# Merging an expert pair's second product with two float16 matmuls, with six product and four row buffers and two additions issued at other places

## The reference, cut to what matters

```python
x = x + xattn(layernorm(x), ctx, mask, Wq, Wk, Wv, Wo)
h = layernorm(x)
topk_idx, topk_w = gate(h)                      # 4 of 32 experts
buf[e, slot] = h rows that chose e              # the first CAP = 128 of them
hid = silu(buf @ w1) * (buf @ w3)
ob = hid @ w2                                   # per expert [128, 512]
out = x + sum(ob rows * topk_w) + (silu(h @ sg) * (h @ su)) @ sd
```

## Time and profile before

| what | value |
|---|---|
| median of 3 runs | 1669.8 us (1669.02 to 1671.42) |
| profiled execution, its own time | 1666.62 us |
| its span | 1664.9 us |
| PE busy | 1617.9 us, 97% of the span, 12194 matmuls and transposes |
| DVE, ACT, POOL busy | 1213.6, 820.1, 818.8 us |
| granted TensorE clock, mean | 0.99 of full speed |

### The profile page before, as it was taken

The page is one execution under the profiler, slowest core; times in us unless marked ns, Lnnn a source line. Parts: engine busy times, 40 slices in busy tenths (PEclk is TensorE's granted clock), DMA queues, the critical chain, the costliest instruction groups (busy, mean ns, idle before and its releaser), DMA issues. The chain is left out here.

```text
span 1664.9 us, 34808 instructions
## 1 busy us (share of the span) xinstructions
PE 1617.9 (97%) x12194; PEld 1155.4 (69%) x12194; DVE 1213.6 (73%) x3508; ACT 820.1 (49%) x2028; POOL 818.8 (49%) x1136
## 2 busy tenths in 40 slices
PE   8999999999999999999999999999999999899975
PEld 5767677777777777767677777777777777555532
DVE  7887676767677776767676778787877766577764
ACT  6664344435343444444443545454554433577763
POOL 3444544545363645454544554646555356344443
PEclk9999999999999999999999999999999999999988
DMA  8754433334343334333433454545454485599984
GB/s 258 175 142 79 83 83 78 83 74 94 71 96 71 87 68 101 69 80 72 90 76 85 96 103 93 112 90 112 92 115 78 97 291 185 140 277 291 299 248 69
DMA packets 394477, 204.12 MB, mean 123 GB/s; under 512 B 347824, under 2 KB 356016, under 8 KB 394304
## 3 DMA queue, kind: packets, MB, share of 16 engines
q1 hardware_dynamic: 380432, 180.27, 44.5%
q0 software_dynamic: 13312, 20.57, 6.4%
q10 hardware_dynamic: 560, 1.05, 0.2%
HBM read 87.15 MB, written 31.36 MB: 71 GB/s over the span
## 5 line engine op out<-in xcount | busy, mean ns | idle before, releaser
L958 ACT ACTIVATE arena<-arena,neg_max 128x256 f32<-128x256 f32 x512 | 253.7, 496 | 378.6 <-DVE neg_max L1265 378.6
L695 POOL TENSOR_SCALAR arena<-arena,prob_scale 128x256 f16<-128x256 f32 x384 | 183.5, 492 | 451.2 <-DVE prob_scale L1274 449.2
L1616 PE MATMUL ps_query<-xn_both,arena 128*128 128x256 f16 x1024 | 279.5, 273 | 1.4 <-DMA xn_both<-xn_half 1.4
L1617 PE MATMUL ps_query<-xn_both,arena 128*128 128x256 f16 x1024 | 279.4, 273 | 0.0
L1618 PE MATMUL ps_query<-xn_both,arena 128*128 128x256 f16 x1024 | 279.4, 273 | 0.0
L1265 DVE CUSTOM_DVE_ANT_0 arena<-ps_score,mask_add 128x256 f32<-128x256 f32 x512 | 186.5, 421 | 126.2 <-PE ps_score L1618 126.2
L1280 DVE SCALAR_TENSOR_TENSOR arena<-arena,prob_scale 128x256 f16<-128x256 f32 x384 | 233.5, 655 | 7.1 <-POOL arena L695 7.1
L1616 PE MATMUL ps_out<-arena,o_t 128*128 128x512 f16 x512 | 194.1, 379 | 2.1 <-DVE o_t L1285 2.1
L1617 PE MATMUL ps_out<-arena,o_t 128*128 128x512 f16 x512 | 194.0, 379 | 0.0
L1618 PE MATMUL ps_out<-arena,o_t 128*128 128x512 f16 x512 | 194.0, 379 | 0.0
L750 POOL DMA_INDIRECT slot_table<-entry,slot_at x128 | 133.9, 1046 | 48.1 <-issue 33.6
(11 more groups left out here) (320 smaller groups left out, 4064.8 us busy)
## 6 DMA issues: line engine op xcount, KB each, us to landing
arena<-w SPq DMA_DIRECT2D x96, 512.0 KB, 6.8
x_in<-x SPq DMA_DIRECT2D x15, 512.0 KB, 3.6
xn_rows<-xn_half SPq DMA_DIRECT2D x15, 512.0 KB, 3.0
out_rows_dram<-x SPq DMA_DIRECT2D x30, 256.0 KB, 2.3
ctx_in<-ctx_t SPq DMA_DIRECT2D x16, 256.0 KB, 3.0
weight_in<-wq SPq DMA_DIRECT2D x8, 512.0 KB, 5.4
weight_in<-wo SPq DMA_DIRECT2D x8, 512.0 KB, 4.7
arena<-arena SPq DMA_TRANSPOSE x256
```

The source lines that it names most:

```text
L695: pool.tensor_scalar(p_rows[:, c, 0, :], probs[:, c, :], prob_scale[:, c:c + 1], 1.0, ALU.mult, ALU.mult).then_inc(norm_hi, 1)
L958: act.activation(probs[:, c, :], probs[:, c, :], ACT.Exp, bias=neg_max[:, c:c + 1], scale=-1.0, accum_out=prob_sum[:, c:c + 1]).then_inc(e ...
L1616: pe.matmul(dst, a.hi, b.hi, start=start and n == 0, stop=False)
L1617: pe.matmul(dst, a.hi, b.lo, start=False, stop=False)
```

## The change

Four edits.

1. **The pair's second product as a float16 pair.** ACT, behind `scale_y` of every odd expert, copies `ps_out[1]` once more into `pair_y.hi`, in float16 and scaled by 16 over `EY_S` (`pair_y` is the attention's `o_t`, idle by then). DVE makes `pair_y.lo` in `pair_rest`, from `ps_out[1]` and `pair_y.hi`, behind `expert_ht_low` of the next even step. The merge is two float16 matmuls, by `hi` and by `lo`, and waits for `pair_lo`; so does `expert_down` of odd experts, which overwrites `ps_out[1]`. The match matrix is float16.
2. **Six product buffers, four row buffers.** `scale_y(e)` waits for the addition of e-6, and gathers run six experts ahead.
3. **Two additions at other places.** `add_shared(1)` stands right behind the load of the slot table, `add_shared(2)` behind two splits further down; both stood behind five gathers.
4. `match` writes its row numbers without the copy at its end (three instructions, not four).

```diff
+PAIR_S = 16.0
...
-        rows_in = [rows.bitcast(F16) for rows in (x_in[0][:, 0, :], x_in[0][:, 1, :], x_in[1][:, 0, :])]
+        rows_in = [rows.bitcast(F16) for rows in (x_in[0][:, 0, :], x_in[0][:, 1, :], x_in[1][:, 0, :], x_in[1][:, 1, :])]
...
         expert_y = [x1[:, t, :] for t in range(TB)] + [
-            xn2_half[:, t, :, :].rearrange("p h d -> p (h d)").bitcast(F32) for t in range(TB)]
+            xn2_half[:, t, :, :].rearrange("p h d -> p (h d)").bitcast(F32) for t in range(TB)] + [
+            both[:, :, :, :].rearrange("p h k t -> p (h k t)")[:, 2 * D:4 * D].bitcast(F32) for both in xn_both]
...
+        pair_y = o_t
...
             def gather(e):
-                if e >= 3:
-                    pool.wait_ge(pe_rows, e - 2)
+                if e >= 4:
+                    pool.wait_ge(pe_rows, e - 3)
...
+            add_shared(1)
             late_split(17)
             pool.wait_ge(in_table, 16)
...
-            for e in range(3):
+            for e in range(4):
                 gather(e)
             for k in (20, 21):
                 late_split(k)
-            for e in range(3, 5):
+            add_shared(2)
+            for e in range(4, 6):
                 gather(e)
             for k in (22, 23):
                 late_split(k)
-            add_shared(1)
-            add_shared(2)
...
-                if e >= 4:
-                    act.wait_ge(added, adds_done["x", e - 4])
-                else:
+                if e >= 6:
+                    act.wait_ge(added, adds_done["x", e - 6])
+                elif e < 4:
...
-                act.activation(expert_y[e % 4], ps_out[e % 2][:, :], ACT.Copy, scale=1.0 / EY_S).then_inc(scaled_y, 1)
+                act.activation(expert_y[e % 6], ps_out[e % 2][:, :], ACT.Copy, scale=1.0 / EY_S).then_inc(scaled_y, 1)
+                if e % 2:
+                    if e > 1:
+                        act.wait_ge(pe_merged, e // 2)
+                    act.activation(pair_y.hi, ps_out[1][:, :], ACT.Copy, scale=PAIR_S / EY_S).then_inc(pair_hi, 1)
...
+            def pair_rest(e):
+                dve.wait_ge(pair_hi, e // 2 + 1)
+                dve.scalar_tensor_tensor(pair_y.lo, ps_out[1][:, :], PAIR_S / EY_S, pair_y.hi, ALU.mult,
+                                         ALU.subtract).then_inc(pair_lo, 1)
...
                     expert_ht_low(e)
+                if e >= 2 and e % 2 == 0:
+                    pair_rest(e - 2)
...
             def merge(e):
                 pe.wait_ge(matched, e // 2 + 1)
-                pe.wait_ge(scaled_y, scaled_at(e + 1))
-                pe.matmul(ps_out[0][:, :], pair_match[e // 2 % 2], expert_y[(e + 1) % 4], start=False, stop=True).then_inc(
-                    pe_merged, 1)
+                pe.wait_ge(pair_lo, e // 2 + 1)
+                pe.matmul(ps_out[0][:, :], pair_match[e // 2 % 2], pair_y.hi, start=False, stop=False)
+                pe.matmul(ps_out[0][:, :], pair_match[e // 2 % 2], pair_y.lo, start=False, stop=True).then_inc(pe_merged, 1)
```

More of the change, by code:

```diff
@@ L254, in build @@
                                  for both in ctx_both))]
-        pair_match = [one_hot[:, :, :, :].rearrange("p t k e -> p (t k e)")[:, n * P:(n + 1) * P] for n in range(2)]
+        pair_match = [one_hot[:, :, :, :].rearrange("p t k e -> p (t k e)").bitcast(F16)[:, n * P:(n + 1) * P]
+                      for n in range(2)]
+        pair_y = o_t
         scratch = picked[:, :, :, :].rearrange("p t k e -> p (t k e)")
-        row_f, to_spare, hits, row_moved = scratch[:, 0:E], scratch[:, E:2 * E], scratch[:, 2 * E:2 * E + 1], \
-            scratch[:, 2 * E + 1:2 * E + 2]
+        row_f, to_spare, hits = scratch[:, 0:E], scratch[:, E:2 * E], scratch[:, 2 * E:2 * E + 1]
         second_rows = scratch[:, 3 * E:3 * E + E // 2].bitcast(U32)
@@ L283, in build @@
         scattered = [signal(f"scattered{n}") for n in range(2)]
-        gathered = [signal(f"gathered{n}") for n in range(3)]
+        gathered = [signal(f"gathered{n}") for n in range(4)]
         in_expert = [signal(f"in_expert{n}") for n in range(AHEAD)]
@@ L317, in build @@
         dve_own, pool_own = signal("dve_own"), signal("pool_own")
-        matched, pe_merged = signal("matched"), signal("pe_merged")
+        matched, pe_merged, pair_hi, pair_lo = (signal(n) for n in ("matched", "pe_merged", "pair_hi", "pair_lo"))
         CONSTS = 14
@@ L755, in gather @@
             def gather(e):
-                if e >= 3:
-                    pool.wait_ge(pe_rows, e - 2)
+                if e >= 4:
+                    pool.wait_ge(pe_rows, e - 3)
                 pool.indirect_dma_start(
-                    rows_in[e % 3], None, xn2_rows, bass.IndirectOffsetOnAxis(ap=table[:, e, 0:1], axis=0),
-                    bounds_check=N + CAP - 1, oob_is_err=True).then_inc(gathered[e % 3], 16)
+                    rows_in[e % 4], None, xn2_rows, bass.IndirectOffsetOnAxis(ap=table[:, e, 0:1], axis=0),
+                    bounds_check=N + CAP - 1, oob_is_err=True).then_inc(gathered[e % 4], 16)
             def add_rows(e):
@@ L768, in add_rows @@
                 pool.indirect_dma_start(
-                    out, bass.IndirectOffsetOnAxis(ap=rows, axis=0), expert_y[e % 4], None,
+                    out, bass.IndirectOffsetOnAxis(ap=rows, axis=0), expert_y[e % 6], None,
                     bounds_check=N + 2 * CAP - 1, oob_is_err=True, compute_op=ALU.add).then_inc(added, 16)
@@ L835, in pool_program @@
             for e in range(E + 2):
-                if e + 5 < E:
-                    gather(e + 5)
+                if e + 6 < E:
+                    gather(e + 6)
                 if e % 2 and e >= 3:
@@ L1431, in match @@
                 dve.wait_ge(*own.now())
-                dve.scalar_tensor_tensor(row_moved, hits, to_spare[:, e + 1:e + 2], row_f[:, e + 1:e + 2], ALU.mult,
-                                         ALU.add).then_inc(*own.up())
-                dve.wait_ge(*own.now())
-                dve.tensor_copy(second_rows[:, m:m + 1], row_moved).then_inc(matched, 1)
+                dve.scalar_tensor_tensor(second_rows[:, m:m + 1], hits, to_spare[:, e + 1:e + 2], row_f[:, e + 1:e + 2],
+                                         ALU.mult, ALU.add).then_inc(matched, 1)
+            def pair_rest(e):
+                dve.wait_ge(pair_hi, e // 2 + 1)
+                dve.scalar_tensor_tensor(pair_y.lo, ps_out[1][:, :], PAIR_S / EY_S, pair_y.hi, ALU.mult,
+                                         ALU.subtract).then_inc(pair_lo, 1)
             dve.wait_ge(consts, CONSTS)
@@ L1587, in dve_program @@
             dve.wait_ge(table_scaled, 2)
-            dve.tensor_scalar(to_spare, row_f, spare_row[:, 0:1], -1.0 / EY_S, ALU.subtract, ALU.mult).then_inc(
+            dve.tensor_scalar(to_spare, row_f, spare_row[:, 0:1], -PAIR_S / EY_S, ALU.subtract, ALU.mult).then_inc(
                 table_scaled, 1)
@@ L1773, in expert_rows @@
             def expert_rows(e):
-                pe.wait_ge(gathered[e % 3], 16 * (e // 3 + 1))
+                pe.wait_ge(gathered[e % 4], 16 * (e // 4 + 1))
                 if e:
@@ L1778, in expert_rows @@
                     pe.wait_ge(placed, B)
-                rows = rows_in[e % 3].rearrange("c (h p k) -> c h k p", h=2, k=KD)
+                rows = rows_in[e % 4].rearrange("c (h p k) -> c h k p", h=2, k=KD)
                 for n in range(2 * KD):
@@ L1813, in expert_down @@
                 pe.wait_ge(expert_lo[2], e + 1)
-                if e >= 2:
+                if e < 2:
+                    pe.wait_ge(x1_done, TB * B)
+                elif e % 2:
+                    pe.wait_ge(pair_lo, e // 2)
+                else:
                     pe.wait_ge(scaled_y, scaled_at(e - 2))
-                else:
-                    pe.wait_ge(x1_done, TB * B)
                 w = expert_w[e % HELD][:, 2 * THIRD:]
```

2 lines of the change are left out of this document (1 added, 1 removed).

## The result

| | before | after |
|---|---|---|
| median | 1669.97 us (17 runs, 1665.25 to 1673.94) | 1673.15 us (17 runs, 1670.66 to 1677.52) |
| ratio of the times | | 1.0023, 95% interval 1.0013 to 1.0032 |
| profiled execution, its span | 1666.62, 1664.9 us | 1673.8, 1672.1 us |
| PE, DVE, ACT, POOL busy | 1617.9, 1213.6, 820.1, 818.8 us | 1610.1, 1220.5, 827.8, 814.6 us |

The changed kernel is 0.23% slower by the ratio, 3.8 us; the two medians lie 3.2 us apart. The forecast was 1672.2 us, 0.14% over the median before; the measured median lies 1 us above it and inside the range. The slowdown is small, but clear of the interval.

What follows compares the result with a forecast made beforehand. PE was taken to bound the expert stage, with POOL's serial chain of additions ending the span. Terms -3.2 (all steps to the end), +0.5 (gathers) and +5.1 (clock) gave +2.4 on 1669.8: 1672.2 us, range 1664.5 to 1681.

Steps and rivals of the forecast that it cites:

- The wait for the shared addition: Steps 1 to 2: PE's stall behind ACT's wait for add_shared(1), with half clock behind it, all goes: -8.0 us.
- The product buffer, the gather and the 1.7 us wait: Near step 24, buffer wait, late gather and half clock go, -13.5 us; half of ACT's second wait, -0.8 us.
- the stalls: PE waits before merges for DVE's rest: 1.75 us with pieces, net +11.3; 2.33 us without, net +9.3.
- the clock: Behind merges: three of five long stalls drop PE to half clock, 1.7 us each, ten short ones none: +5.1 us.
- The last step: Behind scale_y(31), second copy, rest and shorter merge follow one by one in place of the float32 merge: +0.7 us.
- The gathers behind two additions: On POOL, two additions now stand ahead of the first gathers; bounds 0 and 3 us, taken as +0.5 us.
- Rival 3: First gathers land some 3 us late and a clock fall follows: 1676.4 us; chance 0.05.
- The end: Last addition goes out 0.3 us behind ACT's last copy, no longer waiting for the pair before: -3.2 us in all.
- rival 2: The clock falls at most merges of even steps, 1.7 us a fall; ten falls give 1684 us; chance 0.25.
- Rival 1: The clock holds with no falls behind merges: -2.7 us, 1667.1 us; chance 0.33.
- Rival 4: Additions lag so ACT still waits with six buffers and half the 13.5 us stays: 1679 us; chance 0.05.
- the floor at 1664.5: With stalls a fifth shorter and no clock falls, the time reaches 1664.5 us, where the chain of additions stops it.

Runs made afterwards that it cites:

- e1: The kernel before with only add_shared(1) and add_shared(2) issued sooner, where the change issues them; 1668.40 us, ratio 0.9962 to the kernel before.
- e2: The kernel before with only six product and four row buffers, gathers six experts ahead; 1671.74 us, ratio 0.9991 to the kernel before.
- e4: The changed kernel with the float32 merge put back, keeping the buffers and the sooner additions; 1666.68 us, ratio 0.9960 to the kernel before.
- e3: The kernel before with only the float16 pair and its two-matmul merge, buffers and additions as before; 1686.88 us, ratio 1.0079 to the kernel before.
- e5: The changed kernel with ACT's float16 copy ahead of the float32 one and DVE's rest ahead of a weight split; 1662.90 us, 0.9959 of before.
- e7: e5 with the two additions of a pair issued back to back behind the gather; 1661.24 us, ratio 0.9946 to the kernel before.
- e6: The changed kernel with eight unused float16 matmuls on PE ahead of the merges at e = 20 to 30; 1670.71 us, 0.9994 of before.
- e8: e4 with the two additions of a pair issued back to back behind the gather; 1657.16 us, ratio 0.9917 to the kernel before.

## Why the prediction was right, step by step

Each step against the trace of the changed kernel.

*The wait for the shared addition, -8.0.* From step 1 to the merge of step 2: 1434.21 - 1417.80 = 16.41 us. Predicted 14.63 + 1.75 = 16.38. Right. In e1, where it goes alone, PE gains 7.2 us and the time 6, since the chain takes the rest.

*The product buffer, the gather and the 1.7 us wait, -13.5 and -0.8; the stalls, +11.3 and +9.3; the clock, +5.1.* From step 1 to the merge of step 30 it was 1640.54 - 1415.63 = 224.91 us before and is 1648.30 - 1417.80 = 230.50 now: +5.6. The prediction's terms for the same stretch are -8.0 - 13.5 - 0.8 + 11.3 + 9.3 + 1.75 + 5.1 = +5.15. The size is right, three of the four falls lie in this stretch, and they cost 4.7 us. One reading inside the sum is not right: what took the long waits away. I put the -13.5 down to the buffers. In e2 and e4, which have the buffers and not the pair's waits, ACT's long wait for a product buffer is gone, but PE waits 4.16 and 2.80 us for a gather one or two steps further on. In e3, which has the pair's waits and not the buffers, no gather is late, and of the wait for the product buffer 2 us are left on PE. So in the changed kernel the pair's waits, which I counted as a cost, would have taken away most of the 13.5 by themselves, and by these runs it is their doing, not that of the fourth row buffer, that no gather is late. (In e5 and e7, which have the buffers and short waits, one is late by 0.58 and 1.92 us.) The sum came out because the changed kernel has both.

*Stalls of 1.75 and 2.33 us.* Measured 1.82 and 2.23. The order on the two engines was read rightly. In step 22, ACT:

```profile
1590.96 0.60 ACT L1020 ACTIVATE xn_half<-ps_out 128x512 f32<-128x512 f32 x1
1591.45 0.59 ACT L1024 ACTIVATE o_t<-ps_out 128x512 f16<-128x512 f32 x1
1591.93 0.39 ACT L1007 ACTIVATE q_t<-ps_head 128x256 f16<-128x256 f32 x1
```

and DVE:

```profile
1590.98 2.35 DVE L1408 SCALAR_TENSOR_TENSOR arena<-arena 128x1024 f16<-128x1024 f32 x2
1593.25 0.42 DVE L1425 SCALAR_TENSOR_TENSOR q_t<-ps_head,q_t 128x256 f16<-128x256 f32 x1
1593.58 0.68 DVE L1445 SCALAR_TENSOR_TENSOR o_t<-ps_out,o_t 128x512 f16<-128x512 f32 x1
```

ACT's second copy starts 0.49 behind the first and ends at 1592.04. DVE's rest could start then, and starts at 1593.58, behind two splits and `expert_ht_low`. The durations taken from the attention stage, 594 and 690 ns, are 0.59 and 0.68 here.

*The last step, +0.7.* From the start of the odd copy to that of the even one it was 1650.49 - 1648.62 = 1.87 us before and is 1660.14 - 1657.56 = 2.58:

```profile
1657.56 0.60 ACT L1020 ACTIVATE x<-ps_out 128x512 f32<-128x512 f32 x1 [2.02 <-PE ps_out L1631]
1658.05 0.59 ACT L1024 ACTIVATE o_t<-ps_out 128x512 f16<-128x512 f32 x1
1660.14 0.60 ACT L1020 ACTIVATE x<-ps_out 128x512 f32<-128x512 f32 x1 [1.50 <-PE ps_out L1841]
```

+0.71. The size is right, but the durations that I wrote down add up to 0.05 and not to 0.7. Missing among them is the second copy's own 0.59 us: DVE's rest starts only at 1658.68, behind its end.

*The gathers behind two additions, +0.5.* From the table's load to step 1 it was 1415.63 - 1393.01 = 22.62 us and is 1417.80 - 1394.85 = 22.95: +0.3. Rival 3, 3 us late, did not happen.

*The end, -3.2.* The last pair no longer waits for the one before: its odd addition goes out at 1659.01 with ACT named as what it waited for, its even one at 1662.30. **Mis-sized:** I put the last addition 0.3 us behind the end of ACT's last copy; the row says 1662.30 - 1660.74 = 1.56, and e3, whose end is also set by PE, has 1.60. So this step brings 1.9 us and not 3.2.

*The clock, three falls, +5.1.* Four, in steps 20, 22, 26 and 30; one of them behind a stall of 1.83 that I had left at none. One `expert_up` at half clock costs 4.28 - 2.59 = 1.69 us, as the 1.7 taken from the earlier trace rows; the four cost 1.69, 1.51, 1.46 and 1.66, 6.3 in all. With 6.3 for 5.1 and the 1.3 of the end, +2.4 becomes +4.9, and the stretch measures +5.6. The price was read from rows, but the count was a choice between 0 and 15, and that it came near is luck: no row of before gave it, and the same rows left room for the ten of rival 2. Nor is the row of 1.74 us as clean as I took it: PE had stood still for 0.20 us just before, with 0.8 us of work between the two. By the ratio the change costs 3.8 us and not 5.6: the profiled execution is one of many. Its mean granted clock is 0.992, and of the seventeen five have 0.992, eleven 0.993 and one 0.994. A fall is 0.001 of that mean (1.7 of 1672 us), so most of the others spent less time at 1.2 GHz, by about one fall; where, is not shown. e6 removes the falls and with them 0.29%.

*Rivals 1 and 2* differ from the forecast only in the count of falls, and that count was the one thing the trace of before could not give. Rival 1, and the rule of the Trainium skill beside it (TensorE: Matmul & The Clock Gate, HAM oscillation), had every fall excluded; the rows at 1579.77 and 1648.30, 2.23 and 1.83 us of idle PE and a fall behind each, speak against it. *Rival 4*, ACT still waiting for additions, did not happen either: 0.9 us at most.

*That the chain of additions would set the end* if PE got ahead was used for the end and for the floor at 1664.5. The experiments make it the larger finding: e5, with few stalls and no fall before the end, came out at 1662.9, near that floor. The fit that the Trainium skill gives (DMA: Bandwidth & Descriptors, Anatomy of one DMA) would have a transfer of 256 KB back in 2.0 + 0.6 = 2.6 us, an estimate worked out from its figures. These traces do not agree with it for such an addition. In the runs that the chain ends, the last pair is issued 5.9 to 6.2 us behind the second addition of the pair before, and with 1.86 between the two of a pair, pairs follow each other 7.8 to 8.1 us apart there.

## What to carry to other kernels

Before you make an instruction on the busiest engine shorter, write down what it will wait for: here 0.5 us a merge was bought with 1.8 to 2.2 us of waiting, because the two new producers stood behind other work in their engines' orders, and moving them up won most of it back (e5). Removing waits is worth only what the next resource lets through: in e4 16 us gained up to ACT's last copy gave 7 to 9.5 us of time, as the serial chain of additions took over the end, and a change to that chain's order paid on top of it (e8) where more buffers alone (e2) did not. Try each part of a change alone: here a cost (e3) and a gain (e2) took away the same wait, and their sum said nothing about either. And price a small stall on PE with the clock in it: 2.2 us of waiting may cost 3.9.

## What was unexpected of the hardware

The length of a stall does not settle whether the clock falls. In the changed kernel it fell behind three of five stalls of 2.23 us, behind one of 1.83, and behind none of nine of 1.81 to 1.82 in steps that hold a piece. In e3 it fell behind all three of 2.23 to 2.24, behind the one of 1.83 and one of 3.33, again behind none of nine of 1.81 to 1.82, and a stall of 3.08 us left the clock at 1.00:

```profile
1607.54 0.59 PE L1840 MATMUL ps_out<-o_t,one_hot 128*128 128x512 f16 x1 [2.23 <-DVE o_t L1445]
1622.88 0.38 PE L1840 MATMUL ps_out<-o_t,one_hot 128*128 128x512 f16 x1 [3.08 <-DVE o_t L1445]
```

(the duration tells the clock: a float16 matmul of 512 columns is 0.38 where the granted clock is 1.00, 2.4 GHz, and 0.59 to 0.63 where it is at the lower level, 1.2). Where PE had no wait over 0.8 us, in e5 from 1580 to 1630 and in e6 from 1580 to 1648, it stayed at 1.00. The falls behind merges in these two kernels all lie in steps without a piece; whether it is the piece's work that holds the clock was not tried. What decides between 1.00 and a fall at like stalls stays open.

An addition that waits for its copy goes out 0.78 to 0.85 us behind that copy's end, and not the 0.3 that stands between two issues on POOL: 1650.37 - 1649.59 and 1659.01 - 1658.16 in the changed kernel, an even and an odd one. Only the very last addition takes longer, 1.56 us there and 1.60 in e3; why is open.
